# The nine filler products of each stack layer, in a resident kernel of eight transformer blocks, left out

## The chip, the cores and the metric

The kernel runs on one core of a Trainium2 chip. Its time is the device time of one execution in microseconds (us), from launch to end; a profiled execution also has a span, from its first to its last instruction. Each time below is of one core, so no other core's work stands beside it.

## What is computed

Two sequences of 512 tokens with 128 features (`x`) pass through eight blocks, each added to a residual. Blocks 4 and 6 are the two stacks that this case is about: each has six layers of self-attention, cross-attention to a context of 154 tokens, and a feed-forward part. Cut to that:

```python
NL, D, H, DFF = (6, 128, 16, 512)
for i in range(NL):
    xn = _adaln(x, noise_emb, n1_w[i], n1_b[i])          # layer norm, gain and shift
    q, k, v = jnp.split(xn @ qkv_w[i].T, 3, axis=-1)
    x = x + _attn(_rope(q), _rope(k), v, src_mask) @ so_w[i].T
    xn = _adaln(x, noise_emb, n2_w[i], n2_b[i])
    x = x + _attn(_rope(xn @ cq_w[i].T), _rope(context @ ck_w[i].T),
                  context @ cv_w[i].T, ctx_mask) @ co_w[i].T
    xn = _adaln(x, noise_emb, n3_w[i], n3_b[i])
    h = jax.nn.gelu(xn @ f1_w[i].T + f1_b[i], approximate=False)
    x = x + (h @ f2_w[i].T + f2_b[i])
```

The other six blocks (a slot attention, two mixtures of experts, a cross-attention, a feed-forward with adapters, a quantised one) are outside the change.

## The kernel before

Features lie on the 128 partitions and tokens in the free dimension, 512 columns for each of the two sequences b = 0 and b = 1. `x`, the stack's running value `h`, and one layer's weights `w` stay on chip; the next layer's weights are loaded section by section.

A layer is a list of 371 items, `PLACES`, with a place for each item written out by hand. Every engine walks the same list and issues its own part of each item, so that the order on each engine is fixed and the two sequences are interleaved: while the vector engine takes the maxima of one sequence's scores, the other is in its output projections or its feed-forward part. `stack_walk` runs the list for the six layers of a stack. Results go through two rings of PSUM banks: "s" of three banks (scores, projections, `out`, `f2`), which the vector engine empties, and "e" of two double banks (exponentials, `sel`, `center`, `var`, `f1`), which the scalar engine empties.

An item's name is its kind, the sequence b, and for attention a = 0 (self) or 1 (cross). Those that matter here, with the line of the tensor engine's products in the profile:

- `sel` (L531) spreads the softmax denominators; then the scalar engine takes log (L696) and exp (L702), and GpSimd multiplies (L889, raising `att_ready`).
- `out` (L543) is the output projection, which waits for `att_ready`; the vector engine adds it to `h` (L808).
- `center` (L562) subtracts the mean; the scalar engine squares (L708) and copies (L709). `var` (L573) is the mean of the squares; the scalar engine makes the reciprocal root of it (L716, L719) and the vector engine applies it (L817, L820).
- `f1` (L630) is two halves of the first feed-forward product, its gelu is L771 on the scalar engine; `f2` (L645) is the second product, added to `h` in L863.
- `score` is L459 for self-attention and L466 for cross-attention, its maxima L797 and L799 on the vector engine. `proj` (L587) makes queries or keys, which the vector engine (L834, L838), the scalar engine (L729) and GpSimd (L895, L897, L900) split into bf16 parts, and which DMAs (`restack`, L429) stack. The restack DMAs are issued from SyncE's queue, but for two steps of a layer (`ACT_STACKS`) that the scalar engine issues itself, among them the first part of sequence 1's cross-attention queries.

All products here but the scores and exponentials are float32, and each shows as two matmul records in the trace.

`hold` (L354) issues n products of two constants, `center` and `consts`, 128 by 512 in float32, whose result the next product in the same bank overwrites. The dictionary `FILL` says how many stand ahead of which item in a layer; `fill` issues them after the wait for the bank and ahead of the wait for the data. The same helper is called in other blocks as well.

Of the kernel before, what the change touches and what calls it, by code (L numbers as in the profile page):

```python
# [244 lines left out]
def build(nc, dram):  # L245

    with ExitStack() as ctx:
# [20 lines left out]
        center, mean_w, selector, ident = (consts[:, P * i:P * (i + 1)] for i in range(4))  # L268
# [82 lines left out]
        def hold(pe, dst, n):  # L351

            for _ in range(n):
                pe.matmul(dst, center, consts[:, :], start=True, stop=True)  # L354
# [78 lines left out]

        FILL = {("out", 0, 1): 3, ("out", 1, 1): 2, ("f1", 0, 0): 1, ("score", 1, 1, 0, 0): 2, ("center", 0, 2): 1}

        def stack_pe_items(pe, z):
            def fill(it, dst):
                hold(pe, dst, FILL.get(it, 0))  # L440

            def score(it):
                _, b, a, g, n = it
                if it in FILL:
                    pe.wait_ge(s_free, z.room("s", it, 2))
# [101 lines left out]
            def center_h(it):  # L547
                _, b, k = it
                slot, at = z.use("e", it)
                if it in FILL:  # L550
                    pe.wait_ge(e_free, z.room("e", it, 1))
# [13 lines left out]
            def var(it):  # L565
                _, b, k = it
                slot, at = z.use("e", it)
                if it in FILL:
                    pe.wait_ge(e_free, z.room("e", it, 1))
# [2137 lines left out]
```

## Time and profile before

| | us |
|---|---|
| median of three executions | 3533.99 |
| lowest and highest of them | 3525.29, 3542.89 |
| the profiled execution | 3528.05 |
| its span | 3526.2 |

| engine | busy us | share of the span |
|---|---|---|
| tensor engine, products | 2989.9 | 85% |
| tensor engine, weight loads (beside the products) | 1049.5 | 30% |
| vector engine | 2086.3 | 59% |
| scalar engine | 1909.0 | 54% |
| GpSimd | 805.7 | 23% |

The mean granted clock of the tensor engine was 0.947 of full speed. The page's busy times are sums over stages with different limits; what a layer waits for is read in its timeline. There a layer is cut by its four `out` items, which stand apart as groups of four matmul records on L543: in the first stack's first layer they begin at 833.31, 889.77, 909.77 and 960.95 us, and the next layer's first at 1047.54 us.

### The profile page before, as it was taken

Reading aid. Unit: us, or ns where it says so; the run is one execution under the profiler, and the core shown is the slowest. Engines: PE = TensorE matmul, PEld = TensorE weight load, DVE = VectorE, ACT = ScalarE, POOL = GpSimd, SP = SyncE. Lnnn points to the kernel's source line nnn. Section 1 sums busy time; section 2 is a strip of 40 time slices with the busy share of each in tenths; the row PEclk is TensorE's granted clock in tenths of the full one; section 3 lists DMA queues with packets and bytes.
Section 4 is the critical chain, followed back from the end, with each engine's and each line's share of the span. In section 5 each row is a group of like instructions: output and inputs, shape, how many; then the busy total and the mean of one; then the engine's idle time right before and its main releaser. Section 6 shows DMA issues by size and latency. Waiting matters only on the chain.

```text
span 3526.2 us, 44923 instructions
## 1 busy us (share of the span) xinstructions
PE 2989.9 (85%) x15735; PEld 1049.5 (30%) x15735; DVE 2086.3 (59%) x3631; ACT 1909.0 (54%) x2693; POOL 805.7 (23%) x1327
## 2 busy tenths in 40 slices
PE   7998999868888788888888856888888888888878
PEld 3463333222222222222222222222222222222226
DVE  4326777448375664846658266658375674746634
ACT  5433333337566574665647534647566575665642
POOL 0003454502212222222212102212212122212211
PEclk9999999879999999999989977989999999999999
DMA  1100000001110111101011001011110111101020
GB/s 42 55 14 11 1 1 1 11 20 42 33 37 27 42 28 32 45 20 51 23 33 41 22 9 45 21 35 41 35 37 27 36 34 32 43 22 51 19 94 38
DMA packets 125514, 110.11 MB, mean 31 GB/s; under 512 B 49982, under 2 KB 116076, under 8 KB 125292
## 3 DMA queue, kind: packets, MB, share of 16 engines
q1 hardware_dynamic: 114924, 97.80, 9.4%
q10 hardware_dynamic: 10368, 9.44, 0.9%
q8 instruction: 128, 2.10, 0.2%
q14 instruction: 94, 0.77, 0.1%
HBM read 41.96 MB, written 0.52 MB: 12 GB/s over the span
## 4 chain that ended last, share of the span: by engine, by line
PE 62%; DVE 19%; ACT 7%; POOL 5%; issue 4%; ACTq 1%; SPq 1%; DMA 0%; DVEq 0%; POOLq 0%
PE ps L514 11%; DVE arena L797 9%; PE ps L459 6%; PE ps L488 4%; PE ps L645 4%; ACT arena L670 3%; PE ps L587 3%; PE ps L630 3%; PE ps L543 2%; PE ps L531 2%; PE ps L573 2%; DVE arena L799 2%; PE ps L1491 2%; PE ps L522 2%; PE ps L1479 2%
## 5 line engine op out<-in xcount | busy, mean ns | idle before, releaser
L670 ACT ACTIVATE arena<-ps 128x1024 f32<-128x1024 f32 x960 | 936.4, 1024 | 352.5 <-PE ps L488 349.5
L797 DVE TENSOR_REDUCE arena<-ps 128x1 f32<-128x512 f32 x1536 | 965.4, 684 | 173.2 <-PE ps L459 160.7
L514 PE MATMUL ps<-arena 128*32 128x512 f32 x3840 | 512.5, 608 | 21.2 <-ACT arena L670 18.0
L459 PE MATMUL ps<-arena 49*128 49x512 bf16 x1536 | 312.0, 403 | 226.4 <-DVE arena L797 198.6
L488 PE MATMUL ps<-arena 52*128 52x512 bf16 x1920 | 346.1, 387 | 31.8 <-ACT arena L670 27.1
L799 DVE TENSOR_REDUCE arena<-ps 128x3 f32<-128x462 f32 (+1 forms) x576 | 303.4, 580 | 86.8 <-PE ps L466 81.2
L879 POOL TENSOR_TENSOR arena<-arena,zeros 128x16 bf16<-128x16 f32 x192 | 42.3, 220 | 1011.1 <-DVE arena L797 582.5
L459 PEld LDWEIGHTS ps<-arena 49*128 49x128 bf16 x1536 | 75.1, 94 | 557.8 <-DVE arena L797 479.2
L889 POOL TENSOR_TENSOR arena<-arena 128x512 f32<-128x512 f32 x96 | 121.9, 1270 | 450.7 <-ACT arena L702 450.7
L895 POOL TENSOR_TENSOR arena<-arena 128x512 bf16<-128x512 f32 (+1 forms) x84 | 92.4, 1100 | 549.9 <-ACT arena L729 549.9
L808 DVE TENSOR_TENSOR h<-ps,h 128x512 f32<-128x512 f32 x48 | 33.2, 692 | 291.8 <-PE ps L543 291.8
L817 DVE SCALAR_TENSOR_TENSOR tmp<-tmp,arena,rstd 128x512 f32<-128x512 f32 x72 | 54.1, 751 | 255.3 <-ACT rstd L719 253.0
L1551 ACT ACTIVATE arena<-ps 128x1024 f32<-128x1024 f32 x96 | 98.1, 1022 | 167.1 <-DVE ps L1638 132.7
L354 PE MATMUL ps<-consts 128*128 128x512 f32 x336 | 161.9, 607 | 23.7 <-DVE arena L2075 23.7
L488 PEld LDWEIGHTS ps<-arena 52*128 52x128 bf16 x1920 | 87.3, 94 | 315.3 <-ACT arena L670 179.7
L1721 POOL TENSOR_TENSOR arena<-arena 128x1024 f32<-128x1024 f32 x64 | 150.3, 2349 | 36.2 <-ACT arena L1551 34.9
L587 PE MATMUL ps<-xn,w 128*128 128x512 f32 x288 | 145.6, 631 | 7.4 <-DVE xn L820 5.6
L466 PE MATMUL ps<-arena 49*128 49x154 bf16 x1536 | 102.2, 232 | 49.4 <-DVE arena L799 43.7
L834 DVE TENSOR_TENSOR arena<-ps,rope 128x512 f32<-128x512 f32 x144 | 99.6, 692 | 66.1 <-PE ps L587 58.2
L531 PE MATMUL ps<-arena,selector 128*128 128x512 f32 x192 | 106.6, 637 | 37.0 <-ACT arena L689 30.6
L1638 DVE TENSOR_TENSOR ps<-ps,arena 128x1024 f32<-128x1024 f32 x96 | 116.5, 1228 | 36.3 <-PE ps L1479 36.3
L645 PE MATMUL ps<-arena,w 128*128 128x512 f32 x192 | 133.5, 860 | 2.4 <-DVE arena L799 1.2
(383 smaller groups left out, 4280.3 us busy)
## 6 DMA issues: line engine op xcount, KB each, us to landing
arena<-arena SPq DMA_DIRECT2D x720, 64.0 KB
arena<-we_dram SPq DMA_DIRECT2D x24, 578.5 KB, 7.5
arena<-arena ACTq DMA_DIRECT2D x144, 64.0 KB
w<-weights_dram SPq DMA_DIRECT2D x26, 320.0 KB, 3.1
w<-weights_dram SPq DMA_DIRECT2D x13, 512.0 KB, 4.0
arena<-arena SPq DMA_DIRECT2D x384, 6.0 KB
arena<-arena SPq DMA_DIRECT2D x288, 19.2 KB
w<-weights_dram SPq DMA_DIRECT2D x39, 128.0 KB, 2.2
```

The lines of the kernel that those rows point to most:

```text
L354: pe.matmul(dst, center, consts[:, :], start=True, stop=True)
L459: pe.matmul(s_bank(slot + r), qst[b][rows, idx, P * qt:P * (qt + 1)], kst[b][rows, idx, :], start=True, stop=True).then_inc(s_full, 1)
L488: mm = pe.matmul(e_bank(slot)[:, S * r:S * (r + 1)], (kst, kstc)[a][b][rows, 2 * g + p, P * kt:P * (kt + 1)], qst[b][rows, 2 * g + p, :], ...
L514: mm = pe.matmul(bank(7)[32 * j:32 * j + 32, :], v, prob[:, slot, j, :], start=(g % 2 == 0 and kt == 0), stop=(a == 0 and g % 2 == 1 and k ...
L531: pe.matmul(e_bank(slot)[:, 0:S], selector2[:, :], osb[:, e, :], start=True, stop=True)\
L587: pe.matmul(s_bank(slot + i)[:, 0:B * CTX if u == 3 else S], w[:, base + P * i:base + P * (i + 1)], src, start=True, stop=True).then_inc(s ...
L645: mm = pe.matmul(s_bank(slot), w[:, W_F2 + P * t:W_F2 + P * (t + 1)], hid[:, t, :], start=(t == 0), stop=(t == FT - 1))
L670: act.activation(prob[:, chunk_no(b, a, g, kt) % NPROB, 2 * p:2 * p + 2, :], e_bank(slot).rearrange("p (j n) -> p j n", j=2), ACT.Exp, sca ...
L797: op = ve.tensor_reduce(nmax[:, g % 2, r, n:n + 1], s_bank(slot + r), AX.X, ALU.max, negate=True)
L799: op = ve.tensor_reduce(nmax[:, g % 2, r, 3 * n:3 * n + pack(n)], s_bank(slot + r)[:, 0:pack(n) * CTX].rearrange("p (i n) -> p i n", n=CTX ...
L889: gp.tensor_tensor(att[:, b, e, :], osb[:, e, :], rinv[:, e, :], ALU.mult).then_inc(att_ready, 1)
L1721: gp.tensor_tensor(sum2[0:n, :, :], sum2[0:n, :, :], prob2[0:n, j], ALU.add).then_inc(s2["summed"], 1)
```

## The change

The dictionary of fillers is made empty:

```diff
-        FILL = {("out", 0, 1): 3, ("out", 1, 1): 2, ("f1", 0, 0): 1, ("score", 1, 1, 0, 0): 2, ("center", 0, 2): 1}
+        FILL = {}
```

Nine products of a layer go, 108 in the twelve layers of the two stacks. No other instruction is added, removed or moved on any engine. The waits for a bank that a filler carried are now carried by the item behind it. The calls of `hold` in other blocks stay.

On the tensor engine, from the second projection of the cross-attention queries of sequence 1 (L587) to the feed-forward part of sequence 0 (L630), before, with seven of the nine fillers (L354):

```order
L531 MATMUL ps<-arena,selector 128x512
L587 MATMUL ps<-xn,w 128x512 x2
L354 MATMUL ps<-consts 128x512 x3
L543 MATMUL ps<-arena,w 128x512 x2
L354 MATMUL ps<-consts 128x512
L562 MATMUL ps<-h,consts 128x512
L573 MATMUL ps<-sq,consts 128x512
L354 MATMUL ps<-consts 128x512 x2
L466 MATMUL ps<-arena 128x154 x6
L354 MATMUL ps<-consts 128x512
L630 MATMUL ps<-xn,w 128x512 x2
```

And after:

```order
L531 MATMUL ps<-arena,selector 128x512
L587 MATMUL ps<-xn,w 128x512 x2
L543 MATMUL ps<-arena,w 128x512 x2
L562 MATMUL ps<-h,consts 128x512
L573 MATMUL ps<-sq,consts 128x512
L466 MATMUL ps<-arena 128x154 x6
L630 MATMUL ps<-xn,w 128x512 x2
```

The items stand in the same order; only the products between them are gone.

On the same engine some 50 us later, at the cross-attention's output projection of sequence 1, the difference is one row:

```order
 L522 MATMUL ps<-arena 32x512 x8
 L531 MATMUL ps<-arena,selector 128x512
-L354 MATMUL ps<-consts 128x512 x2
 L543 MATMUL ps<-arena,w 128x512 x2
 L459 MATMUL ps<-arena 128x512 x4
```

Here the last two fillers of the layer stood between `sel` and `out`.

## Rows read from the trace of the kernel before

**Rows 1.** The page: granted clock in 40 slices, and the chain by engine.

```profile
PEclk9999999879999999999989977989999999999999
...
PE 62%; DVE 19%; ACT 7%; POOL 5%; issue 4%; ACTq 1%; SPq 1%; DMA 0%; DVEq 0%; POOLq 0%
```

**Rows 2.** All of L354; duration min, median and max in ns.

```profile
L354 PE MATMUL ps<-consts x336: 592/593/1192, 124.5 to 3464.9; 128*128 128x512 f32 x168
```

**Rows 3.** Timeline of all engines, from 905 to 921 us: start, duration, instruction, idle before.

```profile
907.01 1.27 POOL L889 TENSOR_TENSOR arena<-arena 128x512 f32<-128x512 f32 x1 [6.43 <-ACT arena L702]
907.20 2.74 PE L354 MATMUL ps<-consts 128*128 128x512 f32 x6
...
908.86 0.63 ACT L729 ACTIVATE arena<-arena 128x512 bf16<-128x512 f32 x1 [1.93 <-DVE arena L838]
...
909.52 4.32 ACTq L429 DMA_DIRECT2D arena<-arena  x6
...
909.77 1.88 PE L543 MATMUL ps<-arena,w 128*128 128x512 f32 x4
...
911.49 1.02 PE L354 MATMUL ps<-consts 128*128 128x512 f32 x2
...
911.69 0.69 DVE L808 TENSOR_TENSOR h<-ps,h 128x512 f32<-128x512 f32 x1 [2.86 <-PE ps L543]
...
912.44 1.13 PE L562 MATMUL ps<-h,consts 128*128 128x512 f32 x2
913.89 0.60 ACT L708 ACTIVATE sq<-ps 128x512 f32<-128x512 f32 x1 [4.40 <-PE ps L562]
...
914.54 1.12 PE L573 MATMUL ps<-sq,consts 128*128 128x512 f32 x2 [0.98 <-ACT sq L708]
...
915.50 1.88 PE L354 MATMUL ps<-consts 128*128 128x512 f32 x4
...
917.32 0.37 PE L466 MATMUL ps<-arena 49*128 49x154 bf16 x6
...
917.62 1.13 PE L354 MATMUL ps<-consts 128*128 128x512 f32 x2
917.94 0.49 DVE L820 TENSOR_SCALAR xn<-tmp,arena 128x512 f32<-128x512 f32 x1
...
918.58 1.88 PE L630 MATMUL ps<-xn,w 128*128 128x512 f32 x4
```

**Rows 4.** The same view, from 957 to 961 us.

```profile
957.14 1.13 PE L531 MATMUL ps<-arena,selector 128*128 128x512 f32 x2 [1.36 <-ACT arena L689]
...
958.10 1.88 PE L354 MATMUL ps<-consts 128*128 128x512 f32 x4
...
959.64 1.26 POOL L889 TENSOR_TENSOR arena<-arena 128x512 f32<-128x512 f32 x1 [2.49 <-ACT arena L702]
960.95 1.98 PE L543 MATMUL ps<-arena,w 128*128 128x512 f32 x4 [0.97 <-POOL arena L889]
```

**Rows 5.** Timeline of the tensor engine, two items in a stretch at the low clock.

```profile
967.41 2.08 PE L573 MATMUL ps<-sq,consts 128*128 128x512 f32 x2
...
973.92 3.44 PE L630 MATMUL ps<-xn,w 128*128 128x512 f32 x4
```

**Rows 6.** Windows from `out` (1,1) to the next layer's first `out`: busy, clock, DMA.

```profile
960.95:1047.54 86.59, 72.72 (x372) 22.77 (x372) 64.91 (x106) 49.65 (x70) 15.79 (x31) 0.90 0.13 36
1175.13:1257.21 82.08, 67.14 (x372) 20.61 (x372) 64.72 (x106) 49.65 (x70) 15.81 (x31) 0.98 0.13 38
...
1597.66:1682.53 84.87, 69.86 (x371) 21.60 (x372) 64.82 (x106) 49.65 (x70) 15.79 (x31) 0.94 0.13 37
...
sum 841.32, PE 694.27 PEld 214.99 DVE 647.68 ACT 496.52 POOL 158.02; mean PE 69.43 PEld 21.50 DVE 64.77 ACT 49.65 POOL 15.80
```

**Rows 7.** Windows from `out` (0,1) to `out` (1,1), in two layers.

```profile
909.77:960.95 51.18, 42.14 (x217) 14.64 (x216) 21.45 (x36) 25.57 (x36) 16.10 (x27) 0.97 0.17 52
...
1333.47:1386.24 52.77, 43.62 (x217) 15.20 (x215) 21.54 (x36) 25.57 (x36) 16.11 (x27) 0.94 0.17 50
```

**Rows 8.** Windows around a fall of the clock, then one just ahead of another.

```profile
922.60:925.70 3.10, 1.24 (x18) 0.57 (x17) 2.59 (x6) 2.25 (x4) 0.82 (x4) 1.00 0.00 0
925.70:929.10 3.40, 3.22 (x8) 1.36 (x9) 1.41 (x4) 0.00 (x0) 0.82 (x4) 0.50 0.23 60
...
1192.00:1195.40 3.40, 1.22 (x7) 0.29 (x5) 3.40 (x7) 1.01 (x2) 0.00 (x0) 0.99 0.02 4
```

## The prediction, made before the changed kernel was run

> **What bounds the kernel now.** I read the page first. Its chain is 62% tensor engine and 19% vector engine, and the granted clock, nine tenths or more in most of the 40 slices, is 7 or 8 in six of them [rows 1]. So the tensor engine matters twice, by its work and by the speed it is given. The change takes out work that nobody reads, and the question is what that work stood on: the path, or a wait. The reader is to take three views in turn: the timeline of all engines around the fillers, which tells what each filler delays; the timeline of the tensor engine alone, which tells what an item costs at either clock; and windows with the granted clock over whole stages, which tell how much of a lost microsecond reaches the next layer.
>
> **What the fillers cost.** A filler is two records of 592 ns that overlap [rows 2]; six records, three fillers, take 2.74 us [rows 3], so about 0.9 us each and some 97 us for all 108. That is 2.8% of the time, and the most that could ever come back. Taken one by one in the first layer of the first stack:
>
> - Three ahead of `out` (0,1). They run from 907.20 us; GpSimd's product, on which `out` waits, ends at 907.01 + 1.27 = 908.28 us, and `out` begins at 909.77 us when the fillers are done [rows 3]. So `out` is late by about 1.44 us (it follows GpSimd by 0.05 us in [rows 4]).
> - One ahead of `center` (0,2). The vector engine's addition ends at 911.69 + 0.69 = 912.38 us and `center` begins at 912.44 us: this filler is hidden.
> - But what `center` feeds is late for another reason. Its squaring on the scalar engine begins at 913.89 us, and just ahead of it that engine issues six DMAs, from 909.52 us for 4.32 us, to 913.84 us [rows 3]. These hang on L729 at 908.86 us, which comes from the query projection ahead of the fillers. The squaring would begin at 913.89 us even if `center` came 1.4 us earlier. The 1.44 us are given back whole.
> - Two ahead of the cross-attention scores, one ahead of `f1`. `f1` needs the normalised input, ready at 917.94 + 0.49 = 918.43 us, and begins at 918.58 us [rows 3]. Without fillers it could begin about 0.1 us earlier.
> - Two ahead of `out` (1,1). They end near 959.98 us, the engine then waits 0.97 us, and `out` begins at 960.95 us, 0.05 us behind GpSimd's 959.64 + 1.26 us [rows 4]. Nothing comes back.
>
> At an unchanged clock the change is worth 0.1 us a layer, 12 x 0.1 = 1.2 us in all. The cover is the scalar engine's DMA issue in one place and the chain of softmax denominators in the other. If the first cover were not there the bound would be 12 x 1.44 = 17 us.
>
> **What the clock does.** Without fillers two stretches become thin. First, from 908.33 us, where `out` (0,1) would begin, to `f1` at 918.48 us, the engine has `out` 1.88, `center` 1.13, `var` 1.12 and scores 0.37 us: 4.5 us of work in 10.15 us, and behind the end of `out` only 2.6 us in 8.3 us, in pieces. Today it waits 0.98 us in all of it [rows 3]. Second, between the end of L522 at 955.8 us (957.14 less the 1.36 us of idle) and `out` (1,1) at 960.95 us, 5.15 us, there remains `sel` with 1.13 us [rows 4]. What stood ahead of today's falls? From 922.60 to 925.70 us the engine was busy 1.24 of 3.10 us, in short pieces with waits of 0.6 to 0.8 us between, and it fell to 0.50 for the next 3.4 us; from 1192.00 to 1195.40 us it was busy 1.22 of 3.40 us and fell at the end [rows 8]. The new thin stretches are at least as empty for at least as long, so I take it that the clock falls behind both, in every layer.
>
> What a fall costs is read from the same items at the low clock, 0.50 of 2.4 GHz, that is 1.2 GHz: `var` 2.08 us against 1.12, half of `f1` 3.44 us against 1.88 [rows 3, 5].
>
> *Behind the first stretch* lie `var` and both halves of `f1`, on the path: the second half waits only for the first on the engine, `f2` for both, and `out` (1,1) and sequence 1 behind them. All of them at the low clock: 0.96 + 2 x 1.56 = 4.1 us. None: 0. Today's falls in a layer last 3.4 to 10.3 us (3.4 in the second row of [rows 8]; the clock of 0.94 in [rows 7] is 6.3 us in 52.77); some of the fall lies where the engine waits anyway. I take 4.4 us of full work inside it, which loses half: 2.2 us. That a loss there reaches the end of the stage shows in [rows 7]: with 3.1 us at the low clock (2 x 0.03 x 51.18) the stage takes 51.18 us, with 6.3 us 52.77 us, 1.6 us more.
>
> *Behind the second* lies `out` (1,1) itself, then `center`, `var`, the values and `f1` of sequence 1. This stage has a ready experiment in [rows 6]: between ten such pairs of `out`, the clock was 0.98 in five and they took 82.1 to 82.5 us, 0.94 in two and 84.9 us, 0.90 in three and 86.6 to 87.1 us; the mean is 84.13 us. So a stage where the fall comes early takes 4.5 us more than one where it doesn't, at the same work. In addition `out` (1,1) can lose 1.7 us (half of what four records take at the low clock), which none of the ten had. I take half the layers as recovering at once: 82.3 + 1.7 = 84.0 us; and half as the slowest of today with part of `out` on top: 86.8 + 0.7 = 87.5 us. Mean 85.75 us, 1.6 us more than now. Bounds: -0.1 us (84.0 for all) and +4.4 us (88.5 for all).
>
> The sum for a layer is -0.1 + 2.2 + 1.6 = +3.7 us, for twelve +44 us. The profiled execution took 3528.05 us with a span of 3526.2 us, so it would become 3572 us. The median of three runs is 5.9 us above the profiled one, and I forecast the median: 3534 + 44 = **3578 us**, 1.2% slower.
>
> The Trainium skill, "TensorE: Matmul & The Clock Gate", section on HAM oscillation, ties the fall to long idle gaps of the engine. The longest new gaps here are 2.7 us (958.27 to 960.95) and 2.4 us, and the falls of [rows 8] came with gaps under 1 us, so the trace reaches further than that rule. By the rule taken strictly the clock would stay where it is and only the 1.2 us would count. The same page's section on psum-queue depth-cycling has the clock swing with short idles, and [rows 8] agree with that one.
>
> **The rivals.**
>
> *The clock doesn't mind.* The pieces left (1.9, 1.1, 1.1 us) might be enough to hold it: they are long float32 products, whereas the engine ahead of today's falls ran short bf16 ones. Then -1.2 us, 3533 us. Against it: in the second stretch only 1.13 us is left in 5.15. 12%.
>
> *The path follows the tensor engine after all, and the clock stays.* If the scalar engine's DMA issue is not what holds the squaring, or starts earlier with the rest, 1.44 us a layer come back, 3534 - 17 = 3517 us, or a little less with the 0.1. It needs the squaring to begin less than 4 us behind L729, which [rows 3] speak against. 3%.
>
> *Everything low.* The clock falls behind both stretches and doesn't rise before the next thin piece (922 to 926 us, 980 to 984 us). First stage +4.1 us, second +4.4 us, less 0.1: 8.4 us a layer, 101 us, 3635 us. For it: in [rows 6] the low clock held for 17 us of 86.59. Against it: `f1`'s two halves are back-to-back work, and under such work, `f2`'s in [rows 8], the clock was back after 3.4 us. It overtakes the forecast once a fall outlasts both halves. 12%.
>
> **How the numbers follow.** Forecast as worked out, 73%; the others 12, 3 and 12%. The forecast's own range takes the two terms half-way to their bounds: 1.1 and 0.75 us, or 3.15 and 3.0 us, less 0.1; that is +21 to +73 us, 3555 to 3607 us. To hold eight in ten I stretch it down to the unchanged clock, 3533 us, and leave out most of the last rival: 3532 to 3616 us. A measurement of this kernel can tell about 0.5%, 17.7 us: within it lie the unchanged clock, half of the second rival, and the cases of the forecast below its own range (4 in 100): same 0.17; faster 0.02; slower 0.81.
>
> **What would show it.** Right: in the changed kernel's timeline the squaring L708 still begins where the scalar engine's six DMA issues end, although `out` (0,1) and `center` are about 1.4 us earlier against L729; `out` (1,1) still begins 0.05 us behind L889; the granted clock is 0.50 over part of `f1` of sequence 0 in most layers and over part of `out` (1,1) or what follows; the mean clock is under 0.947, near 0.92 to 0.93; the vector engine's busy time is unchanged. Wrong: a mean clock that stays; windows between `out` (0,1) and `out` (1,1) near 51 us; windows from `out` (1,1) on that are no longer than today's mean of 84.13 us because falls only moved from one place to another. The last is the weakest step: when the clock falls also depends on how layers come to lie in time, and a few can be luckier than now.

## The result, and the profile after

The changed kernel takes 3572.68 us (median of four executions, 3567.41 to 3586.78) against 3538.44 us of the kernel before, run beside it. The ratio is 1.0108 with a 95% interval of 1.0064 to 1.0152: 1.1% slower, where 3578 us, 1.2% slower, was forecast. The forecast added 44 us to the 3534 us known then; beside its own kernel before, the change is worth 34 us.

The page of the changed kernel: span, busy times, granted clock in 40 slices, chain by engine, to be held against [rows 1].

```profile
span 3585.0 us, 44491 instructions
...
PE 2960.7 (83%) x15519; PEld 1021.8 (29%) x15519; DVE 2084.7 (58%) x3631; ACT 1909.9 (53%) x2693; POOL 808.0 (23%) x1327
...
PEclk9999999879999898998979977989999998999999
...
PE 61%; DVE 19%; ACT 7%; POOL 5%; issue 4%; SPq 2%; DMA 1%; DVEq 0%; ACTq 0%; POOLq 0%
```

The tensor engine has 216 records less. Taken at the 0.86 us that a filler adds to a row of them (2.74 less 1.88 us, [rows 3]), the 108 were some 93 us of work, and yet the engine's busy time fell by 29 us only, from 2989.9 us: what is left runs slower. The mean granted clock went from 0.947 to 0.924. The other engines' busy times are the same within 3 us.

The profiled execution is the slowest of the four (3586.78 us), and part of its 58.8 us of longer span is not the change: its first `out` begins at 839.95 us in place of 833.31 us, ahead of anything that was edited. The two stacks, from the first to the last `out`, take 1218.2 and 1204.7 us in place of 1188.0 and 1184.2: 50.7 us, or 4.2 us a layer (the last layer of a stack is in this only up to its last `out`). The rest is 6.6 us before them and 1.5 us between and behind. So this execution, with the lowest clock of the four (the two fastest had 0.935), is 14 us above its median, and the profiled one before was 10 us under its own: the stages below show more of a loss than the medians do.

The timeline of the tensor engine after, in the first layer of the first stack, answers to [rows 3]:

```profile
915.07 1.95 PE L543 MATMUL ps<-arena,w 128*128 128x512 f32 x4 [1.07 <-POOL arena L889]
917.80 1.12 PE L562 MATMUL ps<-h,consts 128*128 128x512 f32 x2 [0.78 <-DVE h L808]
921.15 1.43 PE L573 MATMUL ps<-sq,consts 128*128 128x512 f32 x2 [2.23 <-ACT sq L708]
923.79 0.57 PE L466 MATMUL ps<-arena 49*128 49x154 bf16 x6 [1.21 <-DMA arena<-arena]
925.44 3.56 PE L630 MATMUL ps<-xn,w 128*128 128x512 f32 x4 [1.08 <-issue]
...
929.24 1.98 PE L630 MATMUL ps<-xn,w 128*128 128x512 f32 x4
...
934.85 5.40 PE L645 MATMUL ps<-arena,w 128*128 128x512 f32 x8 [0.23 <-DVE arena L799]
```

And of all engines, the scalar engine's rows in the same stretch:

```profile
916.16 4.30 ACTq L429 DMA_DIRECT2D arena<-arena  x6
...
920.50 0.60 ACT L708 ACTIVATE sq<-ps 128x512 f32<-128x512 f32 x1 [4.37 <-issue]
```

`center` ended at 918.92 us, yet the squaring begins at 920.50 us, where the six DMA issues end (916.16 + 4.30 = 920.46). The first half of `f1` takes 3.56 us in place of 1.88.

Windows of the changed kernel: from `out` (1,0) to `out` (0,1); three pieces behind `out` (0,1); then from `out` (0,1) to `out` (1,1) in the first layer and the sum of ten, as in [rows 7].

```profile
896.44:915.07 18.63, 16.54 (x91) 4.76 (x89) 3.62 (x6) 12.51 (x17) 2.55 (x2) 1.00 0.02 5
...
915.07:921.80 6.73, 3.72 (x8) 1.24 (x8) 1.09 (x2) 1.72 (x3) 3.42 (x3) 1.00 0.29 86
921.80:928.70 6.90, 4.61 (x12) 1.44 (x10) 2.33 (x4) 3.29 (x4) 0.00 (x0) 0.51 0.10 31
928.70:935.40 6.70, 4.53 (x34) 1.86 (x34) 4.94 (x10) 3.62 (x5) 0.83 (x4) 1.00 0.00 0
```
```profile
915.07:969.91 54.84, 39.54 (x204) 13.16 (x205) 21.77 (x37) 26.21 (x37) 16.32 (x27) 0.90 0.16 49
...
sum 547.30, PE 393.67 PEld 130.73 DVE 217.69 ACT 262.09 POOL 163.36; mean PE 39.37 PEld 13.07 DVE 21.77 ACT 26.21 POOL 16.34
```

And the windows from `out` (1,1) to the next layer's first, answering to [rows 6], with the stretch at the low clock in one of them:

```profile
969.91:1055.25 85.34, 70.24 (x371) 21.46 (x372) 64.70 (x106) 49.67 (x70) 15.84 (x31) 0.94 0.13 37
1185.94:1275.77 89.83, 76.18 (x372) 23.37 (x372) 64.97 (x106) 49.67 (x70) 15.84 (x31) 0.86 0.12 35
...
sum 874.56, PE 729.87 PEld 223.22 DVE 648.18 ACT 496.69 POOL 158.42; mean PE 72.99 PEld 22.32 DVE 64.82 ACT 49.67 POOL 15.84
```
```profile
1184.60:1205.10 20.50, 16.71 (x34) 5.86 (x34) 10.77 (x17) 5.03 (x8) 1.20 (x1) 0.50 0.04 12
```

`out` (1,1) itself, in these two layers, to be held against the 1.98 us of [rows 4]:

```profile
969.91 3.51 PE L543 MATMUL ps<-arena,w 128*128 128x512 f32 x4 [2.78 <-POOL arena L889]
...
1185.94 3.75 PE L543 MATMUL ps<-arena,w 128*128 128x512 f32 x4 [2.78 <-POOL arena L889]
```

A layer is best followed by the start times of its four `out` items. Means over the ten layers that aren't the last of their stack, in us, with the other kernels that are told of below:

| kernel | (0,0) to (1,0) | (1,0) to (0,1) | (0,1) to (1,1) | (1,1) to (0,0) | clock | median |
|---|---|---|---|---|---|---|
| before | 56.20 | 19.98 | 51.99 | 84.13 | 0.947 | 3538.4 |
| changed | 56.23 | 18.64 | 54.73 | 87.46 | 0.924 | 3572.7 |
| only the two at `out` (1,1) | 56.13 | 18.63 | 54.74 | 83.86 | 0.938 | 3535.4 |
| only the other seven | 56.37 | 19.98 | 52.02 | 87.66 | 0.932 | 3569.2 |
| nine with 32 columns | 56.56 | 18.54 | 54.68 | 85.92 | 0.933 | 3566.5 |
| nine and 35 short ones | 54.81 | 19.98 | 50.55 | 81.19 | 0.970 | 3468.0 |
| nine and 19 short ones | 55.56 | 19.98 | 51.72 | 80.87 | 0.965 | 3499.0 |
| nine and 42 short ones | 54.81 | 19.98 | 50.00 | 81.09 | 0.975 | 3465.6 |
| two and 42 short ones | 54.81 | 18.63 | 53.80 | 80.93 | 0.960 | 3494.3 |
| 42 short ones alone | 54.81 | 18.63 | 53.72 | 80.91 | 0.962 | 3490.3 |
| 42, nine, two in the path | 54.81 | 19.98 | 51.52 | 81.08 | 0.973 | 3486.0 |

The stages and the clock are of the one profiled execution, the median is over all. The kernel before had medians of 3535.2, 3540.1 and 3536.7 us beside the three groups of experiments.

### The profile page after: what moved, and what is told of

Its sections match the earlier page's. It is cut to its first block, busy times and chain, and to the rows that moved or that the text cites. A ratio compares the mean times of both kernels' runs of the same rounds, so it can differ in the third digit from the quotient of the medians.

```text
span 3585.0 us, 44491 instructions
## 1 busy us (share of the span) xinstructions
PE 2960.7 (83%) x15519; PEld 1021.8 (29%) x15519; DVE 2084.7 (58%) x3631; ACT 1909.9 (53%) x2693; POOL 808.0 (23%) x1327
## 4 chain that ended last, share of the span: by engine, by line
PE 61%; DVE 19%; ACT 7%; POOL 5%; issue 4%; SPq 2%; DMA 1%; DVEq 0%; ACTq 0%; POOLq 0%
PE ps L514 11%; DVE arena L797 9%; PE ps L459 5%; PE ps L488 4%; PE ps L630 4%; PE ps L645 3%; ACT arena L670 3%; PE ps L587 3%; PE ps L543 3%; PE ps L531 2%; DVE arena L799 2%; PE ps L1491 2%; PE ps L573 2%; PE ps L522 2%; PE ps L562 2%
## 5 line engine op out<-in xcount | busy, mean ns | idle before, releaser
L587 PE MATMUL ps<-xn,w 128*128 128x512 f32 x288 | 145.2, 629 | 7.3 <-DVE xn L820 5.6
L630 PE MATMUL ps<-xn,w 128*128 128x512 f32 x192 | 131.8, 827 | 21.7 <-issue 21.7
L708 ACT ACTIVATE sq<-ps 128x512 f32<-128x512 f32 x76 | 45.2, 595 | 189.5 <-PE ps L562 136.9
```

The costliest lines, as they stand in the source:

```text
L587: pe.matmul(s_bank(slot + i)[:, 0:B * CTX if u == 3 else S], w[:, base + P * i:base + P * (i + 1)], src, start=True, stop=True).then_inc(s ...
L630: mm = pe.matmul(e_bank(slot)[:, S * i:S * (i + 1)], w[:, W_F1 + P * t:W_F1 + P * (t + 1)], cols(xn, b), start=True, stop=True)
```

## The experiments

The theory is the forecast's: the fillers' time is covered, and they hold the tensor engine's clock. The rivals are that the fillers act in another way, that falls of the clock only move from one place to another, and that the fillers' time was on the path.

### One part of the change at a time

Only the two ahead of `out` (1,1) kept:

```diff
-        FILL = {("out", 0, 1): 3, ("out", 1, 1): 2, ("f1", 0, 0): 1, ("score", 1, 1, 0, 0): 2, ("center", 0, 2): 1}
+        FILL = {("out", 1, 1): 2}
```

> Only the two fillers ahead of out (1,1) are kept, the other seven of a layer are gone. Theory of two separate stages: the stage from out (1,1) stays as before (82 to 87 us, mean 84.1), the stages from out (1,0) to out (1,1) go from 72.0 to 73.3 us as with all nine gone; so 12 x 1.35 = +16 us, ratio 1.005, out (1,1) itself at the high clock in every layer. Rival, that falls only move from one place to the next: the stage from out (1,1) changes as well (over 86 us in most layers although its fillers are there), ratio 1.010 as with all nine gone, or under 1.002 because it shortens.

Measured: 3535.42 us (3526.74 to 3559.85, 12 executions) against 3535.15 us, ratio 1.0015 (0.9994 to 1.0035). Two windows of it, from `out` (0,1) and from `out` (1,1):

```profile
911.76:966.56 54.80, 41.32 (x209) 13.96 (x209) 21.75 (x37) 26.20 (x37) 16.29 (x27) 0.91 0.16 48
```
```profile
966.56:1048.91 82.35, 67.15 (x371) 20.68 (x372) 64.59 (x106) 49.65 (x70) 15.81 (x31) 0.98 0.13 38
```

The stages came as expected (73.4 us for the two around `out` (0,1), 83.9 us from `out` (1,1)), and the profiled execution's stacks took 11.2 us more than before. But that execution, 3552.21 us, is the third longest of twelve, and 9.5 us of it lie behind the stacks; the median hardly moved. So the seven fillers are worth 0.35% at most in this kernel (the end of the interval), less than the 0.5% expected from the stages. A ratio under 1.002 is also what the rival named, but the stage that should have shortened for it did so by 0.27 us only. The nine fastest executions had a mean clock of 0.942 to 0.947, the three slowest, with the profiled one among them, 0.933 to 0.938. Where in a layer the faster ones differ isn't settled: only profiled executions show their stages.

Only the other seven kept:

```diff
-        FILL = {("out", 0, 1): 3, ("out", 1, 1): 2, ("f1", 0, 0): 1, ("score", 1, 1, 0, 0): 2, ("center", 0, 2): 1}
+        FILL = {("out", 0, 1): 3, ("f1", 0, 0): 1, ("score", 1, 1, 0, 0): 2, ("center", 0, 2): 1}
```

> The seven fillers around out (0,1) are kept, the two ahead of out (1,1) are gone. Theory of two separate stages: the stage up to out (1,1) as before (mean 52.0 us), the stage from it 87.5 us as with all nine gone, 12 x 3.3 = +40 us, ratio 1.011. Rival: without the loss in the first stage the falls around out (1,1) come as well placed as before, ratio under 1.005.

Measured: 3569.17 us (3564.84 to 3572.23), ratio 1.0101 (1.0075 to 1.0127), and the sum of its ten stages from `out` (1,1):

```profile
sum 876.60, PE 734.93 PEld 225.15 DVE 648.15 ACT 496.53 POOL 158.08; mean PE 73.49 PEld 22.52 DVE 64.82 ACT 49.65 POOL 15.81
```

That is 87.66 us a stage, and the stage ahead is as before (52.02 us). Two products of nine, ahead of `out` (1,1), carry nearly the whole change, and neither stage took over what the other lost.

### The same instructions with little in them

```diff
             def fill(it, dst):
-                hold(pe, dst, FILL.get(it, 0))
+                for _ in range(FILL.get(it, 0)):
+                    pe.matmul(dst[:, 0:32], center, consts[:, 0:32], start=True, stop=True)
```

> All nine fillers stand where they stood, each with 32 columns in place of 512, so that the instructions, their weight loads and the waits they carry are kept and the work is a sixteenth. If the fillers act by keeping the tensor engine busy and so its clock up: as with all nine gone, ratio 1.008 to 1.014, mean clock 0.925 to 0.935. Rival, that they act by their place in the queue (weights loaded early, waits carried ahead): as before, ratio 0.998 to 1.002, clock 0.947.

Measured: 3566.52 us (3563.62 to 3579.65), ratio 1.0100 (1.0072 to 1.0128), clock 0.933. All nine fillers in their place, by min, median and max in ns:

```profile
L441 PE MATMUL ps<-consts x216: 192/276/422, 911.2 to 3435.3; 128*128 128x32 f32 x108
```

The kernel is as slow as without them, and `out` (1,1) takes 3.36 to 3.78 us in all twelve layers, where it took 1.98 us with the full fillers. So it isn't the place in the queue, the weight loads or the waits that they carry; it is the work in them.

### Is their time covered?

On the scalar engine the six DMA issues are put behind the squaring, with the nine fillers, and then without the four at `out` (0,1) and `center` (0,2) (`FILL` keeps the other five):

```diff
-    ('center',): [[-45, 157, 302], [38, 285, 373]],
+    ('center',): [[-45, 157, 299], [38, 285, 373]],
...
-    ('st', 1): [[67, 71, 73], [79, 80, 81], [299, 300, 301]],
+    ('st', 1): [[67, 71, 73], [79, 80, 81], [302, 300, 301]],
```

> All nine fillers kept; on the scalar engine alone the six DMA issues of the first part of sequence 1's cross-attention queries come behind the squaring and copying of center (0,2) in place of ahead of them. If these issues are what covers the four fillers at out (0,1) and center (0,2): the squaring begins 0.2 us behind the end of center, about 8.2 us behind the start of L587 in place of 8.4, and the log of var now waits for the DMA issues, so that f1 begins about 3 us later against L587 than before; 12 x 3 = 36 us slower. Rival, that something else holds the squaring: it begins where it did and nothing moves.

> As the run with the scalar engine's DMA issues behind the squaring, and the three fillers ahead of out (0,1) and the one ahead of center (0,2) are gone. With the cover away these fillers stand on the path: the squaring begins 1.4 us earlier against L587 than with them (about 6.9 us behind its start), the DMA issues, the log of var and f1 too (before any loss by the clock). Rival, that they never delayed anything behind out (0,1): no difference between the two runs but in out (0,1) itself.

The second query projection (L587) begins at 904.17 us in the first and at 914.26 us in the second of these kernels. The scalar engine's rows with the nine fillers:

```profile
912.29 0.60 ACT L708 ACTIVATE sq<-ps 128x512 f32<-128x512 f32 x1 [4.10 <-PE ps L562]
...
912.98 3.37 ACTq L429 DMA_DIRECT2D arena<-arena  x5
916.46 0.69 ACT L716 ACTIVATE lg<-ps,epst 128x512 f32<-128x512 f32 x1 [3.08 <-issue]
```

And without the four:

```profile
921.12 0.60 ACT L708 ACTIVATE sq<-ps 128x512 f32<-128x512 f32 x1 [2.84 <-PE ps L562]
...
921.80 3.53 ACTq L429 DMA_DIRECT2D arena<-arena  x5
925.44 0.69 ACT L716 ACTIVATE lg<-ps,epst 128x512 f32<-128x512 f32 x1 [3.24 <-issue]
```

The squaring begins 8.12 us behind L587 with the fillers and 6.86 us without: 1.26 us that the fillers now cost, and 1.11 us of it reaches the log of `var` (12.29 and 11.18 us). With the DMA issues in their old place it began 8.41 us (913.89 less 905.48) behind L587 before the change and 8.38 us after it, 920.50 less 912.12. So the scalar engine's DMA issue was the cover of the squaring.

The expectation had `f1` earlier too, before any loss by the clock, and it isn't. The tensor engine's rows of the scores and of `f1` with the fillers:

```profile
918.31 0.37 PE L466 MATMUL ps<-arena 49*128 49x154 bf16 x6 [2.52 <-DMA arena<-arena]
...
919.57 1.88 PE L630 MATMUL ps<-xn,w 128*128 128x512 f32 x4
```

And without the four:

```profile
928.02 0.57 PE L466 MATMUL ps<-arena 49*128 49x154 bf16 x6 [3.42 <-DMA arena<-arena]
928.52 2.08 PE L354 MATMUL ps<-consts 128*128 128x512 f32 x2
930.39 2.34 PE L630 MATMUL ps<-xn,w 128*128 128x512 f32 x4
```

The scores, which stand ahead of `f1` on the engine, wait in both for DMAs, some of which are now issued later, and begin only 0.38 us earlier (13.76 in place of 14.14 us behind L587); then the clock is low (one filler 2.08 us in place of 1.13) and `f1` begins 16.13 us behind L587 in place of 15.40. The first of the two kernels has `f1` 2.3 us later than before (15.40 against 918.58 less 905.48, 13.10 us), where 3 us were expected.

As wholes the two took 3558.84 and 3581.34 us, one execution each (before: 3540.09 us): the first is 18.8 us slower where 36 us were expected. From the first to the last `out` of the two stacks they take 2404.3 and 2405.5 us, against 2372.2 us before: the order of the kernel before is the better one. Of the 22.5 us between the two wholes only 1.2 lie in the stacks, so whether the four fillers pay for themselves without the cover isn't shown.

### More fillers, where the engine waits

If the clock is what the nine buy, then the falls that are left in the kernel before can be bought too. Short fillers, a bf16 record of 512 columns each, go into a bank (7) that holds nothing at these places that is still to be read, at places where the timeline of before shows the engine waiting for the vector engine:

```diff
+        EARLY = {("score", 1, 1, 1, 0): 2, ("score", 1, 1, 1, 1): 3, ("score", 1, 1, 1, 2): 2,
+                 ("score", 0, 0, 0, 1): 3, ("score", 0, 0, 0, 3): 2, ("score", 0, 0, 0, 6): 5,
+                 ("score", 0, 0, 1, 1): 2, ("score", 0, 0, 1, 2): 2, ("score", 0, 0, 1, 3): 3, ("score", 0, 0, 1, 4): 2,
+                 ("score", 1, 0, 1, 3): 3, ("score", 1, 0, 1, 4): 3, ("out", 1, 1): 3}
...
+            def early(it):
+                for _ in range(EARLY.get(it, 0)):
+                    pe.matmul(bank(7), identb[:, :], consts[:, 0:256].bitcast(BF16), start=True, stop=True)
...
             def score(it):
                 _, b, a, g, n = it
+                early(it)
...
             def out(it):
...
                 fill(it, s_bank(slot))
+                early(it)
                 pe.wait_ge(att_ready, z.after("inv", ("inv", b, a, 1), it))
```

> All nine fillers and 32 short ones more in a layer (one bf16 record of 512 columns each, about 0.21 us, into a bank that nobody uses there), two to five at a time where the engine waits 0.6 to 1.9 us for the vector engine ahead of f2 of either sequence, ahead of the first out of a layer, and behind out (1,1). Theory: the 3 to 6 falls of a layer that are left go, each worth 1.1 to 1.6 us, so 12 x 3 to 12 x 7 us, 36 to 84 us faster, ratio 0.976 to 0.990, mean clock over 0.97. Rival: the short ones delay the scores on which the vector engine waits, 0.1 to 0.3 us at each of 12 places, 14 to 43 us slower in itself, and the sum is near 1.000.

(The table has 35 of them; the text left out the three at `out` (1,1).) Measured: 3468.02 us (3463.45 to 3475.70), ratio 0.9821 (0.9794 to 0.9847), clock 0.970: 67 us faster than the 3535.15 us beside it, within what the theory gave. Only those between `out` (1,1) and `f2` of sequence 1, 19 in a layer:

```diff
-        EARLY = {("score", 1, 1, 1, 0): 2, ("score", 1, 1, 1, 1): 3, ("score", 1, 1, 1, 2): 2,
-                 ("score", 0, 0, 0, 1): 3, ("score", 0, 0, 0, 3): 2, ("score", 0, 0, 0, 6): 5,
-                 ("score", 0, 0, 1, 1): 2, ("score", 0, 0, 1, 2): 2, ("score", 0, 0, 1, 3): 3, ("score", 0, 0, 1, 4): 2,
-                 ("score", 1, 0, 1, 3): 3, ("score", 1, 0, 1, 4): 3, ("out", 1, 1): 3}
+        EARLY = {("score", 0, 0, 0, 1): 3, ("score", 0, 0, 0, 3): 2, ("score", 0, 0, 0, 6): 5,
+                 ("score", 0, 0, 1, 1): 2, ("score", 0, 0, 1, 2): 2, ("score", 0, 0, 1, 3): 3, ("score", 0, 0, 1, 4): 2}
```

> The nine fillers, and of the short ones only those between out (1,1) and f2 of sequence 1, 19 in a layer. Separate stages: only the stage from out (1,1) changes, from 84.1 to 81.2 us, 12 x 2.9 = 35 us faster, ratio 0.990; out (0,0) and the stage behind out (0,1) lose as before. Rival, that falls only move on: they come back between f2 and the next out (0,0), ratio over 0.996.

Measured: 3499.02 us, ratio 0.9895 (0.9876 to 0.9915): the stage from `out` (1,1) takes 80.87 us, the others lost nothing (the rival had the falls come back there). And seven more than the 35:

```diff
-                 ("score", 1, 0, 1, 3): 3, ("score", 1, 0, 1, 4): 3, ("out", 1, 1): 3}
+                 ("score", 1, 0, 1, 3): 3, ("score", 1, 0, 1, 4): 3, ("out", 1, 1): 3,
+                 ("score", 1, 1, 2, 1): 2, ("score", 1, 1, 2, 2): 2, ("score", 0, 0, 1, 6): 2, ("score", 0, 0, 1, 7): 1}
```

> All fillers of the run with 35 short ones, and seven short ones more in a layer, ahead of the scores behind either f2, where the last falls inside the stacks lie (six stages of twenty, 1.2 to 1.7 us each). Theory: these go, 9 to 12 us more, ratio 0.978 to 0.980, clock 0.975. Rival: they delay scores and give 0 to 3 us back.

Measured: **3465.62 us** (3465.18 to 3473.73), ratio 0.9802 (0.9782 to 0.9823), clock 0.975, the fastest version found: 2.0% under the kernel before, 3% under the changed one, with more work in it than either. The seven last ones gave 2.4 us between medians of two groups, less than the 9 to 12 us expected, within the rival's 0 to 3 us and within what the medians tell. One profiled execution of each suggests that they act: from `out` (0,1), 50.00 us in place of 50.55, with one fall of the clock left in the ten stages where there were five. The two windows of it, a layer's stage from `out` (1,1) and from `out` (0,1):

```profile
1385.16:1465.93 80.77, 72.76 (x400) 21.97 (x400) 64.60 (x106) 49.67 (x70) 15.85 (x31) 1.00 0.14 39
920.69:970.47 49.78, 44.19 (x231) 15.04 (x229) 21.36 (x36) 25.58 (x36) 16.14 (x27) 1.00 0.18 54
```

The tensor engine is busy for 72.76 us where it was for 67.14 us in the best stage of [rows 6], and the stage is 1.3 us shorter at a clock of 1.00 in place of 0.98.

### The nine fillers, with the clock high elsewhere

From the kernel with 42 short ones, the seven taken out, then all nine, and then two long ones added where no wait covers them:

```diff
-        FILL = {("out", 0, 1): 3, ("out", 1, 1): 2, ("f1", 0, 0): 1, ("score", 1, 1, 0, 0): 2, ("center", 0, 2): 1}
+        FILL = {("out", 1, 1): 2}
```
```diff
-        FILL = {("out", 0, 1): 3, ("out", 1, 1): 2, ("f1", 0, 0): 1, ("score", 1, 1, 0, 0): 2, ("center", 0, 2): 1}
+        FILL = {}
```
```diff
-        FILL = {("out", 0, 1): 3, ("out", 1, 1): 2, ("f1", 0, 0): 1, ("score", 1, 1, 0, 0): 2, ("center", 0, 2): 1}
+        FILL = {("out", 0, 1): 3, ("out", 1, 1): 2, ("f1", 0, 0): 1, ("f1", 0, 1): 2, ("score", 1, 1, 0, 0): 2, ("center", 0, 2): 1}
```

> The kernel with 42 short fillers in a layer, less the seven long ones around out (0,1); the two ahead of out (1,1) stay. With the clock high everywhere else this shows what the seven are worth alone. If their time is covered and only the clock matters: the stages from out (1,0) to out (1,1) go from 70.0 to 71.4 or 72.5 us (falls under var and f1, as when only the two were kept), 12 x 1.4 to 2.5 = 17 to 30 us slower than the kernel with 42, the stage from out (1,1) still 80.8 to 81.9 us. Rival, that the seven cost their 0.9 us each on the path: faster by up to 12 x 1.4 us.

> The 42 short fillers of a layer and none of the nine long ones. Ahead of out (1,1) only three short ones (0.6 us) are left in the 5.2 us thin stretch. If the nine act by the clock: falls at out (1,1) and under f1 come back, some shortened by the short fillers behind them; 12 x 3 to 12 x 6 us slower than the kernel with 42 and all nine, ratio 0.990 to 1.001. Rival, that the short ones are enough: ratio 0.980.

> The kernel with 42 short and nine long fillers, and two long ones more ahead of the second half of f1 of sequence 0, where the engine doesn't wait and the path runs over it. Price of a filler that no wait covers: 2 x 0.86 = 1.7 us a layer, 21 us over twelve, against the kernel with 42; ratio 0.986. Rival, that the vector engine's maxima cover them: no difference.

Measured: 3494.31 us (ratio 0.9884, 0.9861 to 0.9907), 3490.29 us (0.9876, 0.9852 to 0.9900) and 3485.98 us (0.9858, 0.9836 to 0.9880). A window from `out` (0,1) of the first of the three, where the one above had a clock of 1.00:

```profile
909.73:963.74 54.01, 44.11 (x222) 14.53 (x222) 21.75 (x37) 26.20 (x37) 16.32 (x27) 0.91 0.17 49
```

Without the seven the two stages around `out` (0,1) take 72.43 us in place of 69.98: 2.45 us a layer, 29 us in twelve, and 28.7 us is the difference of the medians, at the upper end of what was expected. Without any of the nine it is no worse, 24.7 us over the kernel with 42 where 36 to 72 were expected, and neither the theory's falls at `out` (1,1) nor the rival's 0.980 came: the three short ones ahead of `out` (1,1), 0.6 us of work, keep that stage at 80.9 us, so the two long ones there are not needed once something stands in their place. And two fillers in the path cost 1.52 us a layer in the profiled execution, and 20.4 us between the medians.

## Why the prediction was right, and where its terms were off

**Whether the fillers' time is on the path.** Right for this kernel. After the change `out` (0,1) begins 1.34 us earlier (18.64 in place of 19.98 us), as forecast with 1.44, and the squaring doesn't: it stands 8.38 us behind the query projection in place of 8.41. With the DMA issues moved away, the squaring comes 1.26 us earlier without the fillers, but `f1` doesn't, because in that order the scores ahead of it wait for DMAs. So the 17 us that the prediction gave as the bound without this cover were not seen in any run. `out` (1,1) follows GpSimd as before. The 0.1 us at `f1` can't be seen apart, since `var` ahead of it already runs at the low clock (1.43 in place of 1.12 us). Where no wait covers them, two fillers cost 1.5 us a layer.

**The clock falls behind both thin stretches.** Right, in all twelve layers: the mean clock went from 0.947 to 0.924, the low stretch of the first layer has a part of `var`, the scores and the first half of `f1` in it, and `out` (1,1) took 3.40 to 3.75 us. That it is the clock and no other effect of the fillers is shown by the nine with 32 columns: the instructions and their waits are there, and the same item takes as long as with none.

**The first stage, +2.1 us.** The size was right at the place where it was read: `f2` of sequence 0 begins 19.8 us behind `out` (0,1) in the first layer, after 18.63 us from `out` (1,0), 38.4 us in all in place of 36.5 (so in eight of the twelve layers), and 39.5 us in the four with the longer fall. But the stage ends only 1.40 us later (73.37 in place of 71.97). The missing step is `f2` itself: before the change a fall of its own stood under it in every layer, and it took 5.1 to 6.6 us; after it 5.4 us in nine layers and 3.7 us in three. Before, in a layer of the longer kind, and after, in the same layer of the changed kernel:

```profile
1349.98 6.55 PE L645 MATMUL ps<-arena,w 128*128 128x512 f32 x8
```
```profile
1371.09 3.70 PE L645 MATMUL ps<-arena,w 128*128 128x512 f32 x8 [0.24 <-DVE arena L799]
```

So in three of the twelve layers the later fall didn't come behind the longer earlier one. The medians say still less for this term: with only the two fillers at `out` (1,1) kept, the ratio was 1.0015 (0.9994 to 1.0035), which is 0 to 1.0 us a layer. With the later fall filled up in the kernel of 42 short ones, the seven are worth 2.45 us, near the 2.1 of the term: it was sized for a stage without a fall of its own.

**The second stage, +1.6 us.** The mechanism was right and the size too small: +3.3 us, from 84.13 to 87.46. I took half the layers as recovering at once (84.0 us); the five that did took 85.2 to 85.5 us, since a second, short fall came under `f1` of sequence 1. And I took the others at 87.5 us; they took 88.4 to 90.1 us, with 13.6 to 20.5 us at the low clock without a break, longer than any fall in these stages before. Four of them passed the 88.5 us that I had set as the bound for all.

**The sum.** 3.7 us a layer forecast, 4.8 us in ten layers of the profiled execution; but that execution is the slowest of its four, and by the medians (34 us) the change is worth 2.9 us a layer. By the medians of its parts nearly all of it is in the second term: without the two at `out` (1,1) 34 us, or 2.8 us a layer where 1.6 was forecast, and without the seven 0.3 us in all (12 us by the end of the interval), where 25 us (12 x 2.1) were forecast. The two terms were off in opposite ways, and the kernel before came out 4.4 us above the 3534 us that the forecast stood on. That the time came within 6 us of the forecast is in part luck.

**The rule of the Trainium skill** that was weighed, "TensorE: Matmul & The Clock Gate", HAM oscillation, by which only long idle gaps matter: by it nothing would have been lost. In the changed kernel the longest idle times at the two falls were 2.23 and 2.78 us, and just ahead of the falls in [rows 8] 0.8 us, so this trace disagrees with it. It agrees with the Trainium skill's section on psum-queue depth-cycling, on the same page, where frequent short idles make the clock swing. The nine with 32 columns leave 2.32 us ahead of an `out` (1,1) in place of 2.78, and the clock falls as if they weren't there.

**The rivals.** The unchanged clock (3533 us) and the path that follows the tensor engine (3517 us) fell. "Everything low" (3635 us) was too high, though four stages from `out` (1,1), with 20.5 us at the low clock, behaved like it.

## What to carry to other kernels

A product that nobody reads is not waste when the engine would wait anyway and the products behind it are on the path: price it by what stands behind it at either clock, and put it only where the timeline shows a wait that ends later than the filler does. When fillers are already there, look for the falls that are left; here they were worth some 70 us, twice what the nine had bought. And count a term at the end of its stage, not at its item, because one fall can take the place of another.

## What the runs showed of the hardware that was not expected

With the clock at 1.00 a stage of the stack becomes the same in most layers (80.75 or 80.76 us from `out` (1,1) in six of the ten with 35 short fillers, 54.80 or 54.81 us in all ten for the first stage; two more without a fall took 81.06 and 81.57 us), where it ranged from 82.08 to 87.08 us before: most of the difference between layers of the same work was the clock.

A float32 product of 32 columns took 276 ns by the median record, 192 ns at the least, against 592 ns for 512 columns [rows 2]. Its weight load takes 192 ns by the median. A sixteenth of the columns took nearly half of the time.

The profiled executions differ in parts that no version touched: the stretch from the last `out` to the end took 128.2 to 131.8 us in ten of them and 139.3 to 140.8 us in three, and the first `out` began between 831.98 and 845.91 us, with the same code ahead of it. What makes these differences isn't shown; they are as large as the smaller effects above, so a part of a layer is better compared by its stages than by the whole time.
